# All four score tiles of the causal attention at once, in one burst of each step

## What is computed

```
x = x + L0_xattn(layernorm(x), ctx)      # 16 heads of 8
x = x + L0_ffn(layernorm(x))             # 8 experts of 512, top 2, gelu
x = x + L1_xattn(layernorm(x), ctx)      # two attentions and a feed-forward
x = x + L1_ffn(layernorm(x))             # 32 experts of 64, top 6, silu

def L1_xattn(inputs, ctx):
    att = head(inputs, inputs, inputs, Wk1, Wq1, Wv1, causal)   # one head, 512 x 512
    norm = layer_norm(att + inputs)
    att2 = head(ctx, ctx, att, Wk2, Wq2, Wv2, no mask)          # 512 x 154
    norm2 = layer_norm(att2 + norm)
    ff = leaky_relu(norm2 @ W1 + b1, 0.2) @ W2 + b2
    return relu(layer_norm(ff + norm2))
```

## Time and profile before

| | us |
|---|---|
| median of 3 runs (lowest, highest) | 727.61 (726.37, 727.87) |
| the profiled execution | 726.31 |
| its span | 724.4 |
| TensorE busy | 622.6 (86%) |
| VectorE busy | 426.0 (59%) |
| ScalarE busy | 338.6 (47%) |
| GpSimd busy | 121.1 (17%) |
| mean granted clock of TensorE | 0.987 |

### The profile page before, as it was taken

How to read it: one execution, slowest core, us unless ns; L and a number is a source line. 1 busy time by engine, 2 the same in 40 slices (tenths; PEclk the granted TensorE clock), 3 DMA queues, 4 the chain that set the end, 5 groups by cost and what they waited for, 6 DMA issues and landing times. The chain is left out here.

```text
span 724.4 us, 8192 instructions
## 1 busy us (share of the span) xinstructions
PE 622.6 (86%) x2608; PEld 395.7 (55%) x2608; DVE 426.0 (59%) x1276; ACT 338.6 (47%) x591; POOL 121.1 (17%) x132
## 2 busy tenths in 40 slices
PE   1688888998999988898989898698779878979997
PEld 1454545553565555564556556365546545655664
DVE  4678887775131336562574535658667687557554
ACT  0356565665555466644854466553445213232221
POOL 6112221010022212222212222242000110000000
PEclk9999999999999999999999999999899999999999
DMA  6000003000000000001000000300000000000000
GB/s 232 22 15 8 16 1 123 2 1 1 15 2 0 1 7 1 1 0 66 0 1 0 1 0 8 116 1 0 1 0 1 15 1 0 16 0 1 15 1 14
DMA packets 8058, 12.85 MB, mean 18 GB/s; under 512 B 1105, under 2 KB 6737, under 8 KB 7633
## 3 DMA queue, kind: packets, MB, share of 16 engines
q1 hardware_dynamic: 8016, 12.34, 5.0%
HBM read 11.29 MB, written 1.05 MB: 17 GB/s over the span
## 5 line engine op out<-in xcount | busy, mean ns | idle before, releaser
L1239 PE MATMUL ps<-xThi,w1s 128*128 128x512 f32 x256 | 146.9, 574 | 2.4 <-DVE h L1199 1.2
L1443 PE MATMUL ps<-h,w2s 128*128 128x512 f32 x256 | 126.3, 595 | 1.4 <-DVE ty L1036 1.4
L722 ACT ACTIVATE h<-ps,early 128x512 f32<-128x512 f32 x128 | 87.2, 687 | 85.0 <-PE ps L1241 83.2
L1241 PE MATMUL ps<-xTlo,w1s 128*128 128x512 f32 x256 | 101.8, 398 | 0.0
L1240 PE MATMUL ps<-xThi,w1s 128*128 128x512 f32 x256 | 101.6, 397 | 0.0
L818 ACT ACTIVATE s<-ps 128x512 f32<-128x512 f32 x68 | 40.6, 598 | 124.8 <-PE ps L1241 121.4
L1199 DVE TENSOR_TENSOR h<-s,ps 128x512 f32<-128x512 f32 x68 | 46.6, 685 | 58.0 <-PE ps L1241 41.5
L947 DVE TENSOR_REDUCE NM<-ps 128x2 f32<-128x308 f32 x128 | 58.2, 476 | 24.1 <-PE ps L1311 18.9
L589 POOL TENSOR_TENSOR acc_o<-acc_o,ty 128x512 f32<-128x512 f32 x32 | 42.3, 1322 | 174.2 <-DVE ty L1036 174.2
L1239 PEld LDWEIGHTS ps<-xThi,w1s 128*128 128x128 f32 x256 | 49.3, 193 | 36.7 <-issue 26.1
L1634 PE MATMUL ps<-h,w2s 128*128 128x512 f32 x128 | 66.2, 599 | 0.5 <-DVE h L1204 0.5
(11 more groups left out here) (277 smaller groups left out, 992.4 us busy)
## 6 DMA issues: line engine op xcount, KB each, us to landing
w2s<-w_dram SPq DMA_DIRECT2D x2, 2048.0 KB, 9.3
raw<-gu_dram SPq DMA_DIRECT2D x4, 512.0 KB, 4.5
x_in<-x_dram SPq DMA_DIRECT2D x4, 256.0 KB, 2.8
w2s<-dn_dram SPq DMA_DIRECT2D x1, 1024.0 KB, 4.7
out_dram<-ty SPq DMA_DIRECT2D x4, 256.0 KB, 2.3
late<-late_dram SPq DMA_DIRECT2D x1, 608.5 KB, 8.8
...
```

The source lines that it names most:

```text
L722: nc.scalar.activation(h32[:, c % HR, :], bank[c % 2], ACT.Gelu, bias=b1T[:, c:c + 1]).then_inc(b_gelu.sem, 1)
L1239: M(dst, w[0], xThi[:, x, :], start=start, stop=False)
L1241: return M(dst, w[0], xTlo[:, x, :], start=False, stop=stop)
L1443: M(bank[2], w2s[:, c * P:(c + 1) * P], h32[:, c % HR, :], start=(c % 4 == 0), stop=(c % 4 == 3)).then_inc(b_y.sem, 1)
```

## The change

- The four score matmuls stand in a row at step 5.8, in the order of tiles 2, 0, 3, 1 (`TILES`): tile 3 in RING[0], tiles 2 and 0 side by side in RING[1], tile 1 in ACC. ACC still holds V1's products until ACT has copied them, so the scores now wait for that copy too.
- DVE does mask, maximum and scaling for all four tiles in a row at step 6.4; ACT does the four exponentials in a row at step 7.6. P1 and PN1 hold 1280 packed columns in place of two buffers of 512.
- DVE then takes one reciprocal of z1 (128 x 4) in place of four, and the four scalings in a row (step 9.9).
- The ten transposes stand in a row at step 10.8, into RING[0], RING[1] and MISC; ACT copies the four results in a row at step 11.3; the products with V follow from step 12.2 on, 0.3 steps apart.
- Every later step of stage C, on PE, ACT, DVE and POOL, is planned 1.3 steps earlier (2.3 planned us, 2.5 for the last batch).

The core of the diff (left out are the other times that lose 1.3 and the signals' declarations):

```diff
+def causal(i):
+    return (i + 1) * P
+
+
+def causal_part(t, i):
+    return t[:, sum(map(causal, range(i))):sum(map(causal, range(i + 1)))]
+
+
+
+TILES = [2, 0, 3, 1]
...
-    P1 = sb("P1", [P, 2, S])
-    PN1 = sb("PN1", [P, 2, S])
+
+    P1 = sb("P1", [P, sum(causal(i) for i in range(NT))])
+    PN1 = sb("PN1", [P, P1.shape[1]])
...
+    def score_tile(i):
+        return {0: RING[1][:, 3 * P:4 * P], 1: ACC[:, 0:2 * P], 2: RING[1][:, 0:3 * P], 3: RING[0]}[i]
+
+    def turned(i):
+        return {0: RING[0][:, 3 * P:4 * P], 1: RING[1][:, 0:2 * P], 2: RING[0][:, 0:3 * P], 3: MISC}[i]
...
-            def move_pt(i):
-
-                act.wait_ge(c_pt_ps.sem, c_pt_ps.at(b, i + 1))
-                copy(PT[:, 0:i + 1, i * P:(i + 1) * P], four(MISC)[:, 0:i + 1, :]).then_inc(c_pt.sem, 1)
...
-            for pair in range(2):
-                p = 6 + 3 * pair
-                yield at(p + 1.8)
-                for i in (2 * pair, 2 * pair + 1):
-                    w = (i + 1) * P
-                    act.wait_ge(c_nb.sem, c_nb.at(b, i + 1))
-
-                    if b or i >= 2:
-                        act.wait_ge(c_pn.sem, c_pn.at(b, max(0, i - 1)))
-                    nc.scalar.activation(P1[:, i % 2, 0:w], RING[i % 2][:, 0:w], ACT.Exp, bias=nb1[:, i:i + 1],
-                                         scale=scale1, accum_out=z1[:, i:i + 1]).then_inc(c_p.sem, 1)
-                yield at(p + 3.7)
-                move_pt(2 * pair)
-                yield at(p + 4.6)
-                move_pt(2 * pair + 1)
-            yield at(16.2)
+            yield at(7.6)
+            for k, i in enumerate(TILES):
+                act.wait_ge(c_nb.sem, c_nb.at(b, max(k + 1, 2)))
+                if b:
+                    act.wait_ge(c_pn.sem, c_pn.at(b, 0))
+                nc.scalar.activation(causal_part(P1, i), score_tile(i), ACT.Exp, bias=nb1[:, i:i + 1],
+                                     scale=scale1, accum_out=z1[:, i:i + 1]).then_inc(c_p.sem, 1)
+            yield at(11.3)
+            act.wait_ge(c_pt_ps.sem, c_pt_ps.at(b, 1))
+            for i in range(NT):
+                src = turned(i).rearrange("p (k q) -> p k q", q=P)
+                copy(PT[:, 0:i + 1, i * P:(i + 1) * P], src).then_inc(c_pt.sem, 1)
+            yield at(14.9)
...
-            def scale_rows(i):
-
-                w = (i + 1) * P
-                dve.wait_ge(c_p.sem, c_p.at(b, i + 1))
-                V.reciprocal(r1[:, i:i + 1], z1[:, i:i + 1]).then_inc(c_r.sem, 1)
-                dve.wait_ge(c_r.sem, c_r.at(b, i + 1))
-
-                if b or i >= 2:
-                    dve.wait_ge(c_pt_ps.sem, c_pt_ps.at(b, max(0, i - 1)))
-                V.tensor_scalar(PN1[:, i % 2, 0:w], P1[:, i % 2, 0:w], r1[:, i:i + 1], None, ALU.mult).then_inc(c_pn.sem, 1)
-
-            for pair in range(2):
-                p = 6 + 3 * pair
-                yield at(p + 0.8)
-                for i in (2 * pair, 2 * pair + 1):
-                    w = (i + 1) * P
-                    dve.wait_ge(c_s_ps.sem, c_s_ps.at(b, i + 1))
-                    diag = RING[i % 2][:, i * P:w]
-                    V.tensor_tensor(diag, diag, trimask, ALU.add).then_inc(c_mx.sem, 1)
-                    dve.wait_ge(c_mx.sem, c_mx.at(b, 2 * i + 1))
-                    V.tensor_reduce(nm1[:, i:i + 1], RING[i % 2][:, 0:w], AX.X, ALU.max, negate=True).then_inc(c_mx.sem, 1)
-                    dve.wait_ge(c_mx.sem, c_mx.at(b, 2 * i + 2))
-                    V.tensor_scalar(nb1[:, i:i + 1], nm1[:, i:i + 1], scale1, None, ALU.mult).then_inc(c_nb.sem, 1)
-                yield at(p + 2.5)
-                scale_rows(2 * pair)
-                scale_rows(2 * pair + 1)
-            yield at(15)
+            yield at(6.4)
+            for k, i in enumerate(TILES):
+                dve.wait_ge(c_s_ps.sem, c_s_ps.at(b, max(k + 1, 2)))
+                diag = score_tile(i)[:, i * P:causal(i)]
+                V.tensor_tensor(diag, diag, trimask, ALU.add).then_inc(c_mx.sem, 1)
+                dve.wait_ge(c_mx.sem, c_mx.at(b, 2 * k + 1))
+                V.tensor_reduce(nm1[:, i:i + 1], score_tile(i), AX.X, ALU.max, negate=True).then_inc(c_mx.sem, 1)
+                dve.wait_ge(c_mx.sem, c_mx.at(b, 2 * k + 2))
+                V.tensor_scalar(nb1[:, i:i + 1], nm1[:, i:i + 1], scale1, None, ALU.mult).then_inc(c_nb.sem, 1)
+            yield at(9.9)
+            dve.wait_ge(c_p.sem, c_p.at(b, NT))
+            V.reciprocal(r1[:], z1[:]).then_inc(c_r.sem, 1)
+            dve.wait_ge(c_r.sem, c_r.at(b, 1))
+            if b:
+                dve.wait_ge(c_pt_ps.sem, c_pt_ps.at(b, 0))
+            for i in range(NT):
+                V.tensor_scalar(causal_part(PN1, i), causal_part(P1, i), r1[:, i:i + 1], None, ALU.mult).then_inc(c_pn.sem, 1)
+            yield at(13.7)
...
-            def turn(i):
-
-                pe.wait_ge(c_pn.sem, c_pn.at(b, i + 1))
-                if b or i:
-                    pe.wait_ge(c_pt.sem, c_pt.at(b, i))
+            yield at(5.8)
+            pe.wait_ge(c_qv.sem, c_qv.at(b, 2))
+            for i in TILES:
+                M(score_tile(i), QT1[:, i * P:causal(i)], xiT[:, 0:causal(i)], start=True, stop=True).then_inc(c_s_ps.sem, 1)
+            yield at(10.8)
+            pe.wait_ge(c_pn.sem, c_pn.at(b, NT))
+            for i in range(NT):
                 for kc in range(i + 1):
-                    last = nc.tensor.transpose(MISC[:, kc * P:(kc + 1) * P], PN1[:, i % 2, kc * P:(kc + 1) * P], ident)
-                last.then_inc(c_pt_ps.sem, 1)
-
-            def attend(i):
+                    q = slice(kc * P, (kc + 1) * P)
+                    last = nc.tensor.transpose(turned(i)[:, q], causal_part(PN1, i)[:, q], ident)
+            last.then_inc(c_pt_ps.sem, 1)
+            for i in range(NT):
+                yield at(12.2 + 0.3 * i)
                 pe.wait_ge(c_pt.sem, c_pt.at(b, i + 1))
                 for kc in range(i + 1):
                     last = M(four(ACC)[:, i, :], PT[:, kc, i * P:(i + 1) * P], V1[:, kc, :], start=(kc == 0), stop=(kc == i))
-                return last
-
-            def tiles(pair):
-                p = 6 + 3 * pair
-                for i in (2 * pair, 2 * pair + 1):
-                    yield at(p + 0.1 * (i % 2))
-                    w = (i + 1) * P
-
-                    if b or i >= 2:
-                        pe.wait_ge(c_p.sem, c_p.at(b, max(0, i - 1)))
-                    M(RING[i % 2][:, 0:w], QT1[:, i * P:w], xiT[:, 0:w], start=True, stop=True).then_inc(c_s_ps.sem, 1)
-                for i in (2 * pair, 2 * pair + 1):
-                    yield at(p + 3.3 + 0.9 * (i % 2))
-                    turn(i)
-                for i in (2 * pair, 2 * pair + 1):
-                    yield at(p + 4.7 + 0.5 * (i % 2))
-                    if i == 0:
-                        pe.wait_ge(c_qv.sem, c_qv.at(b, 2))
-                    last = attend(i)
-                if pair == 1:
-                    last.then_inc(c_att_ps.sem, 1)
-
-            yield from by_time(tiles(0), tiles(1))
-            yield at(15.5)
+            last.then_inc(c_att_ps.sem, 1)
+            yield at(14.2)
```

54 lines of the change are left out of this document (27 added, 27 removed).

## The result

The changed kernel takes 750.27 us (median of four runs, 747.69 to 752.68) beside 727.74 for the kernel before (four runs, 726.37 to 728.78). The ratio is **1.0315**, 95% interval 1.029 to 1.0339. The sign of the forecast was right, its size was not: 735.0 was said, with a range of 723 to 741. The profiled execution took 747.69 us, with a span of 745.8 against 724.4.

What follows compares the result with a forecast made beforehand. TensorE, busy 622.6 of 724.4 us, was taken to bound the kernel. Terms 7.7 - 0.5 - 1.5 + 1.7 = +7.4 on 726.31 gave 733.7, said as 735.0 because the median lies 1.3 higher; range 723 to 741.

Steps and rivals of the forecast that it cites:

- The critical pair: Batches 0 and 1: a chunk's first matmul waits for ACT's GELU behind the exponentials; new idle about 2.85 us.
- the first half: Batches 0 and 1, around the burst: new idle opens, old idles of 0.60 and 0.99 go; +1.25 us each.
- The second half: Batches 0 and 1, later steps drawn 1.3 steps closer trade queue places: +2.6 us each, between 0.5 and 4.5.
- four places: Queue trades in batches 0 and 1: xn +0.9, lg +0.9, transposes of PN2 +0.7, routing's exp before P2T's copy +0.3.
- place 3: Transposes of PN2 in batches 0 and 1 lose 1.4 us of cover; their wait of 1.57 becomes 2.3, +0.7.
- Batch 2: New idle replaces two old ones, +0.66; waits for PN2 and ty shrink, -0.93; total -0.5 us (-4 to +3).
- Batch 3: Gate logits come 4.2 us later behind the exponentials, but TensorE is only 0.6 behind later; -1.5 us (-5 to +4).
- The clock: Each new TensorE idle can cost 0 to 1.7 us by half clock; one stretch taken for batches 0 and 1, +1.7.
- Rival 1: TensorE sees the saved table pair in all batches, new idle staying under 1.59: -9.5, about 718 us; chance 0.08.
- Rival 2: Routing waits of batches 2 and 3 shrink, giving the loss back: -4.6, about 723 us; chance 0.12.
- Rival 3: All later shifts in batches 0 and 1 find slack: +0.5, about 728 us; chance 0.12.
- Rival 4: The clock falls after each of the four bursts, 4 x 1.7 us: +12.5, about 740 us; chance 0.18.

Runs made afterwards that it cites:

- The burst alone: The changed kernel with every later step of stage C back at its old time, only scores to products with V staying changed: 735.28 us, ratio 1.0104.
- the middle: The kernel before with stage C's later steps planned 1.3 steps earlier, except the last four (from the second feed-forward product on): 733.02 us, ratio 1.0067.
- the tail alone: The kernel before with only stage C's last four steps (second feed-forward product, sum, third layer norm) planned 1.3 steps earlier: 750.58 us, ratio 1.0311.
- the tail put back: The changed kernel with only stage C's last four steps (second feed-forward product, sum, third layer norm) back at their old times: 737.45 us, ratio 1.014.

## Why the prediction was wrong

**What bounds the kernel** held. Every microsecond of the difference is in TensorE's idle time or clock, and busy shares of the other engines hardly moved (VectorE 421.0 against the 426.0 of the earlier trace rows, ACT 336.4 against 338.6).

**The critical pair and the first half** held, in place and nearly in size. Where a start is compared, 0.36 is taken off it, by which the profile of after runs late already at 259.46 (259.10 before). The F was forecast at 274.75 and stands at 274.67. Its idle was forecast at 2.85 and is 2.54, as TensorE reached it a little later than by the walk. Of the F that stood at 283.70, +1.25 was forecast; it is +2.83, and 1.7 of that is the stretch at half clock (276 to 279), which the forecast had as a term of its own. Without it +1.1, of which 0.5 are the transposes of att (285.08 after), which the shift put ahead of this F. The burst alone shows the same on a whole period: idle 8.59 against 7.70, +0.9.

**The second half is the step that failed.** It was said that "Everything behind is drawn 1.3 steps (2.3 us of the plan) closer", and "four places" were counted, the last of them the copy of P2T at about 302. These four were sized fairly to high: +2.6 was forecast, and the middle has 2.1 and 2.4 of idle alone (periods of batches 0 and 1) but 1.7 and 1.4 on top of the burst, with 2.3 in place 3 as forecast, while lg, put at 1.5, measured 0.27 and xn 0.64 for 0.9. But the shift goes on to stage C's last step, and the walk stopped ahead of the third layer norm (318.75 to 325.75 in VectorE's rows above). Its steps on VectorE and GpSimd moved too, past a ty of stage B that stayed where it was. That costs 3.53 of idle less some 0.5 at the acc_o wait behind it (1.29 to 0.75), or 3.1 a batch by the tail alone, **10 us in the whole span that stood in no term of the sum and in no rival**. The range left no room for it: its upper end was made from the clock alone.

**Batch 2** was forecast at -0.5 and is -1.37, but that is luck: its idle is +0.5, and 1.9 us are clock, for which it had no term. In the idle two errors nearly cancel. The new idle is 2.54 for 2.74, as said. The wait for PN was put at 3.7 by a PN of 2.74 us; it is nil, since PN runs ahead of GpSimd's product now and takes 0.80. With the tail put back the batch thus has 2.6 us less idle. The tail then gives back 3.1.

**Batch 3** was forecast at -1.5 in (-5 to +4) and is +5.97 with the last experts. The logits wait 4.63, as forecast (4 to 6), and two of the later waits did go. The idle of the whole stretch is +0.36 where -1.5 was said, within its bounds; the +5.6 are the clock. Two of its stretches (607 to 614 and 669 to 675, 3.4 us of work lost in each) stand at idles in the last experts that the kernel before has nearly the same at full clock (3.92 at 610.55 for 3.69 at 591.51, 1.40 at 667.33 for 1.41 at 647.45).

**The clock** was forecast at +1.7 and is +9.3. This term was sized wrongly by its rule: it gave a price to new idles alone. Old idles lose or win it too, as the kernel with three matmuls more and the one with two routing times moved show. What rows could give was a bound, not a value: the kernel before has thirteen idles of 1.5 us or more from 290 on, most of them followed by a full clock, and a stretch at half costs 1.7 to 3.4 us wherever it comes.

Put together, idle was forecast at +5.7 and is +1.3 without the tail and +11.4 with it, and the clock was forecast at +1.7 and is +7.4 in busy time without the tail and +10.0 with it. So that burst and middle alone land near the 735.0 of the forecast (737.45) is luck too: their idle was forecast 4.4 us too high and the clock some 6 too low.

**The rivals.** Rival 1 (the table loads saved are what TensorE sees) fell: ACT has 33 loads for 36, as the order said, and each still takes 1.28 us, but ACT's block ahead of the next GELU grew by 1.24 us of exponentials and TensorE waits 2.54. The rule of the Trainium skill's page ScalarE: Activation LUTs, section Table sets: the hidden batching unit, would have given some 10 us by the forecast's estimate; no run shows them. What the second burst had cost TensorE, 1.59 us of idle a batch, did go, and the 2.54 outweigh it. Rival 2 (the routing gives it back) was half right: the wait of batch 2 went, the time did not fall. Rival 3 (the second half finds slack) fell by the middle alone, a ratio of 1.0067. Rival 4 (the clock falls after each burst) had the right kind of loss: the burst alone has it behind each of the bursts of batches 0 to 2, the whole change only behind that of batch 0. It still gives 740, the tail being in none of its terms.

**What stays open.** Why the tail alone loses more to the clock (24.7) than the whole change (19.2) is open, and with one profiled execution each it may be no more than what differs from one execution to the next. The runs can't say which idles will be hit in a new version. Why burst and middle together cost less idle than their sum was not looked into either.
